# Projection of the second attention as three products of fp32r halves, and a ring of MLP weight pieces with five places

## The chip, the cores and the metric

The kernel runs on one core of a Trainium2 chip. A core has five engines that work at the same time, each through its own list of instructions: TensorE (PE, matmuls and the loads of their weights), VectorE (DVE), ScalarE (ACT), GpSimd (POOL) and SyncE (SP, which here only issues DMAs). They meet through semaphores. The metric is the time on the device of one execution, in microseconds, as the median of some runs.

## The reference

Two layers of gated cross-attention and feed-forward on x, 4 batches of 1024 tokens with 256 features:

```python
x = x + jnp.tanh(g_xattn[0]) * _L0_xattn_ref(_layernorm(x, axis=-1), ctx_1024, ...)   # both ways, with a gate
x = x + jnp.tanh(g_ffn[0]) * _L0_ffn_ref(_layernorm(x, axis=-1), Wr, Wi, Wo)           # 8 experts, the best 2
x = x + jnp.tanh(g_xattn[1]) * _L1_xattn_ref(_layernorm(x, axis=-1), ctx_1024, mask, W, b)
x = x + jnp.tanh(g_ffn[1]) * _L1_ffn_ref(_layernorm(x, axis=-1), w1_w, w1_s, ...)      # 256 -> 1024 -> 1024 -> 1024 -> 256
```

The change is in the third line, the second attention:

```python
x_proj = jax.nn.relu(jnp.einsum('bxd,ed->bxe', x, W) + b)
y_proj = jax.nn.relu(jnp.einsum('byd,ed->bye', y, W) + b)
scores = jnp.einsum('bxd,byd->bxy', x_proj, y_proj)
att = jax.nn.softmax(jnp.where(y_mask[:, None, :], -jnp.inf, scores), axis=-1)
return jnp.einsum('bxy,byd->bxd', att, y)
```

and, through the ring, in the loads of the weights of the fourth line.

## The kernel before

The 4096 tokens are 32 tiles of 128, and 8 groups of 4 tiles (512 tokens). The kernel goes through four stages: A the first attention of all batches; B the experts of the first batch (groups 0 and 1), with all experts' products; C, inside B's last pass and inside the MLP, the second attention of one group at a time; D the MLP, group by group, n = 0 to 7. The experts of the other three batches run inside stage D as well: in groups n = 0, 2, 4 the tokens of the next batch are ranked by expert and their rows scattered to DRAM by GpSimd, loaded again sorted, and multiplied; in groups n = 1, 3, 5 and at their start the results are gathered and added.

Everything in stage D is one list per engine, written out by hand. A group on TensorE is: 8 blocks for the first layers (c = 0 to 7), 16 blocks t = 0 to 15 for the two hidden layers (t = 8 * layer + c, 16 matmuls each), and the output layer. Between blocks stand the pieces of other work. `turn_after(n)` gives the block `at` behind which the second attention of group n + 1 begins: 1 in groups 0, 2, 4, 6, and 5 in groups 1, 3, 5. `c_turn` (transposes of the normalised rows) comes after block `at`, `c_project` after `at` + 1, `c_scores_T` after `at` + 2 and so on. ScalarE's list has its copy out of PSUM (`c_turn`, x_norm_c_T, L1344) after block `at`, VectorE's list the maximum and the update.

The matmuls of the MLP are products of fp32r halves: a value is split into a high part, rounded to fp32r, and a low part, the rest. The weights are small whole numbers that fp32r holds exactly, so the MLP needs 2 products. `c_project` (L889 to L895) is one product of fp32 matmuls with the weight w1t and the transposed rows xcT, 4 matmuls of 128x512. It waits for ScalarE's two copies (semaphore xTc_r).

In groups 0, 2 and 4 VectorE has, in its list, `r_coef` after block t = 0, `r_rank` after t = 1 (L1981 to L2007: a copy of the ranks, then some twenty small instructions, each waiting for the one before; the last one writes slots_of_tokens, for which GpSimd's scatters wait), and `r_tiles` after t = 3.

The MLP's weights are 22 pieces of 512 KB a group. `mlp_ring` has six places (RING); GpSimd loads piece r (`load_piece`, L2210) when the piece that used the place has been read, in its own list, between which stand the scatters (in front of the loads of steps 6 to 9 in groups 0, 2, 4), the update of x (`add`, step 20) and the gathers (at the end of groups 0, 2, 4, and at step 8 of groups 1, 3, 5). In stage B all 22 pieces are examined once by ScalarE (are the weights exact in fp32r?): the first 22 - RING through a buffer of their own that SyncE fills, the last RING in the ring.

Stage B's last pass (`b_last_pass`) has 16 products of experts i on TensorE; VectorE adds their results in 8 steps m (`b_add`). The second attention of group 0 runs through it: `c_turn` after i = 4, `c_project` after i = 6.

Of the kernel before, what the change touches and what calls it, by code (L numbers as in the profile page):

```python
# [27 lines left out]
F32 = mybir.dt.float32  # L28
F32R = mybir.dt.float32r
# [4 lines left out]
ALU = mybir.AluOpType  # L34
# [3 lines left out]
P = 128  # L38
B, S, D, L = 4, 1024, 256, 77
KC = D // P  # L40
# [4 lines left out]
GN = G * P  # L45
# [3 lines left out]
BL = B * L  # L49
NW = (2 * KC + 2 * HC) * HID + HC * D  # L50
PIECE = 1024
RING = 6
ND = 2
NSB = B - 1
EB = 23
# [24 lines left out]
def program(nc, d):  # L80

    ctx = ExitStack()
    with ctx:
# [4 lines left out]
        cursor = {k: v[0] for k, v in room.items()}  # L88
        bytes_of = {U8: 1, U16: 2, BF16: 2}

        def place(region, name, shape, dt=F32, at=None):
            size = int(np.prod(shape[1:])) * bytes_of.get(dt, 4)
            size = -(-size // 32) * 32
            start = cursor[region] if at is None else at
            assert start + size <= room[region][1], (name, start + size)
            cursor[region] = start + size
            return nc.alloc_sbuf_tensor_at(name, shape, dt, offset=base + start)

        def sem(name):
            return ctx.enter_context(nc.semaphore(name))  # L100
# [38 lines left out]
                    at=cursor["weights"] - 2 * KC * BL * 4 + B * 2 * D * 4)  # L139
# [21 lines left out]

        mlp_ring = place("weights", "mlp_pieces", [P, RING, PIECE], F32R, at=wi_at)
        assert NW % PIECE == 0

        xs = place("weights", "slot_rows", [P, 2, CHUNK, D])
        xm = place("weights", "x_norm_of_batch", [P, JT, D], at=cursor["weights"] - 2 * CHUNK * D * 4)
        ys = place("weights", "expert_rows", [P, 2, CHUNK, D])
# [1 line left out]
        xsh = place("weights", "slot_rows_T_high", [P, 2, KC, 2 * P], F32R)  # L169
        xmT = place("weights", "x_norm_T", [P, 2, KC, 2 * P], at=cursor["weights"] - 2 * KC * 2 * P * 4)  # L170
        xsl = place("weights", "slot_rows_T_low", [P, 2, KC, 2 * P], F32R)
        wrb = place("weights", "router_of_batch", [P, KC, E])
        rlg = place("weights", "batch_logits", [P, JT, 2 * E])
        rtop = place("weights", "batch_top8", [P, JT, E])
# [105 lines left out]
        xdl_at = cursor["work"]  # L280
# [4 lines left out]

        xnc = place("work", "x_norm_c", [P, G, D], at=xdh_at)
        xpT = place("work", "x_projected_T", [P, KC, GN], at=xdh_at)
        xcT = place("work", "x_norm_c_T", [P, KC, GN], at=xdl_at)
        scT = place("work", "scores_c_T", [L, GN], at=xdl_at)
        PT = place("work", "probs_c_T", [L, GN], at=ud_at)  # L290
        EC = place("work", "probs_c", [P, G, L])
        w1t = place("work", "context_weight", [P, KC, D])
# [3 lines left out]
        ps = ctx.enter_context(nc.psum_tensor("psum", [P, 8, 512], F32))  # L296
# [85 lines left out]
        yb_r = sem("context_projected_copied")  # L382
        tpc = sem("x_transposed_c_in_psum")
        xnc_r = sem("x_normalised_c_ready")
        xTc_r = sem("x_transposed_c_saved")
        xupc = sem("x_updated_c")
        stats_c = sem("ln_stats_c_ready")
        inv_c = sem("ln_rstd_c_ready")
# [135 lines left out]
        def slot_of(n, piece):  # L524

            return (NCHECK * n + piece) % RING

# [71 lines left out]
        def _(pe):  # L599
            mm = pe.matmul  # L600
# [286 lines left out]
                    transpose_pair(xnc, pair, tpc)  # L887

            def c_project(c):  # L889
                pe.wait_ge(xTc_r, 2 * c + 2)  # L890
                for m in range(KC):
                    for k in range(KC):
                        last = mm(ps[:, 2 + m, :], w1t[:, k, m * P:(m + 1) * P], xcT[:, k, :],  # L893
                                  start=(k == 0), stop=(k == KC - 1))
                    last.then_inc(xp_ps, 1)  # L895

            def c_scores_T(c, b):
# [283 lines left out]
        def _(act):  # L1181
# [159 lines left out]
            def c_turn(c):  # L1341
                for pair in range(2):
                    act.wait_ge(tpc, 1 + pair + 2 * c)
                    act.activation(xcT[:, :, 2 * pair * P:(2 * pair + 2) * P],  # L1344
                                   ps[:, pair, :].rearrange("p (k c) -> p k c", k=KC), ACT.Copy).then_inc(xTc_r, 1)

            def c_project(c):
# [168 lines left out]
        def _(dve):  # L1516
# [342 lines left out]
            def c_norm(c):  # L1859
                dve.wait_ge(inv, INV_A + 1 + c)  # L1860
                for j in range(G):
                    normalise(G * c + j, xnc[:, j, :], xnc_r)

            def c_max(c):
                dve.wait_ge(sb_ps, c + 1)
                dve.tensor_reduce(nmc[:], ps[:, 3, 0:G * L].rearrange("p (j c) -> p j c", j=G), X, ALU.max,
                                  negate=True).then_inc(mc_r, 1)
# [40 lines left out]
            def b_last_pass(g, s):  # L1908

                b_end(g - 1)  # L1910
                c_batch(0)
                for m in range(G * E // 4):
                    b_add(g, s, m)
                    if m == 0:
                        c_norm(0)
                    if m == 3:
                        b_measure(g, 0)
                    if m == 4:
                        c_max(0)
                    if m == 6:  # L1920
                        c_update(0)
                        c_stats(0)
                check_weights()
# [7 lines left out]
            st.mark(dve.memset(rwant[:], FAR))  # L1931
            for t in (Mz, M2, M4, Mc, t1, t2, t4, t8):
                st.mark(dve.memset(t[:], 0.0))
            b_last_pass(ND - 1, 1)


# [110 lines left out]
            def stage_d(short):  # L2047
# [29 lines left out]
                def group(n, b, fetch):  # L2077

                    s, at, a = routed_in(n), turn_after(n), added_in(n)
# [19 lines left out]
                    for layer, (full, part, rest) in enumerate(((hb_f, hb_h, hb_l), (ha_f, ha_h, ha_l))):  # L2099
                        for c in range(HC):  # L2100
                            low(c, full, part, rest, 3 * HC * n + HC * (layer + 1) + c + 1)
                            t = HC * layer + c
# [23 lines left out]
                                    measure_rows(n + 2)  # L2126
                            if b is None:
                                continue
                            if t == at + 3:
                                c_max(n + 1)  # L2130
                            if t == at + 7:
# [220 lines left out]
```

## Time and profile before

| | |
|---|---|
| median of 3 runs | 1082.88 us (1081.75 to 1084.19) |
| profiled execution, own time | 1084.55 us |
| its span | 1082.6 us |
| TensorE busy | 1026.4 us (95%) |
| VectorE busy | 506.4 us (47%) |
| ScalarE busy | 479.9 us (44%) |
| GpSimd busy | 305.6 us (28%) |
| mean granted clock of TensorE | 0.979 |

The profile is one execution, so its own time stands beside the median of the runs. Busy time of TensorE is that of records that overlap; where matmuls follow each other, the distance of their starts says what one costs. The stages in the span: A to about 165 us, B to about 250 us, the MLP stage D from 255 us to the end.

### The profile page before, as it was taken

To read this page: it belongs to the slowest core of one execution; us is meant where nothing else is said; L and a number is where in the kernel's file an instruction comes from. 1 tells how busy PE (TensorE), PEld (TensorE's weight loads), DVE (VectorE), ACT (ScalarE), POOL (GpSimd) and SP (SyncE) were. 2 spreads that over 40 slices of the span, in tenths; PEclk is the share of its full clock that TensorE was granted. 3 is DMA by queue.
4 is the path that set the end of the run, shared out by engine and by line. 5 is a ranking of instruction groups with operands and counts; after the bars stand their busy time and mean duration, and the time that the engine had idled before them with its cause. 6 is when DMAs were issued, how large, how long until landed. Compare 5 with 4: busy or idle time off the path is not lost.

```text
span 1082.6 us, 14392 instructions
## 1 busy us (share of the span) xinstructions
PE 1026.4 (95%) x5218; PEld 831.1 (77%) x5218; DVE 506.4 (47%) x1391; ACT 479.9 (44%) x877; POOL 305.6 (28%) x432
## 2 busy tenths in 40 slices
PE   7989998897999999999999999999999999999996
PEld 4757776665778987886789878867898788788885
DVE  6567766746633362555333624553336245133311
ACT  1345442643544453445444544454445345443431
POOL 0025553311161154222611442225114422012111
PEclk9989998998999999999999999999999999999999
DMA  9930001641266365342663744436637544344540
GB/s 333 375 104 2 2 3 57 220 153 40 83 213 225 137 214 156 117 136 88 224 228 117 228 147 125 125 94 234 210 129 222 156 121 152 117 128 145 152 139 22
DMA packets 44276, 158.93 MB, mean 147 GB/s; under 512 B 6448, under 2 KB 6832, under 8 KB 43306
## 3 DMA queue, kind: packets, MB, share of 16 engines
q0 software_dynamic: 29952, 104.88, 31.1%
q1 hardware_dynamic: 10826, 40.63, 10.9%
q10 hardware_dynamic: 3424, 12.45, 2.9%
q8 instruction: 45, 0.74, 0.3%
q14 instruction: 29, 0.24, 0.1%
HBM read 138.01 MB, written 29.36 MB: 155 GB/s over the span
## 4 chain that ended last, share of the span: by engine, by line
PE 75%; DVE 7%; POOL 6%; ACT 4%; issue 4%; DMA 3%; DVEq 0%; POOLq 0%; ACTq 0%
PE psum L987 48%; POOL slots L2227 4%; PE psum L870 2%; DMA slot_rows<-slots 2%; PE psum L893 2%; PE psum L1064 2%; PE psum L1066 2%; PE psum L1065 2%; PE psum L1040 1%; PE psum L692 1%; PE psum L668 1%; PE psum L706 1%; PE psum L880 1%; PE psum L722 1%; PE psum L605 1%
## 5 line engine op out<-in xcount | busy, mean ns | idle before, releaser
L2214 POOL DMA_DIRECT2D mlp_pieces<-in_mlp x176 | 96.9, 557 | 446.6 <-PE psum L987 440.2
L987 PE MATMUL psum<-hidden_a_high,mlp_pieces 128*128 128x512 f32 x512 | 208.0, 406 | 5.3 <-DVE hidden_a_low L2059 5.3
L987 PE MATMUL psum<-hidden_b_high,mlp_pieces 128*128 128x512 f32 x512 | 202.9, 396 | 0.0
L987 PE MATMUL psum<-hidden_a_low,mlp_pieces 128*128 128x512 f32 x512 | 201.5, 394 | 0.0
L987 PE MATMUL psum<-hidden_b_low,mlp_pieces 128*128 128x512 f32 x512 | 199.7, 390 | 0.0
L2059 DVE TENSOR_TENSOR hidden_a_low<-hidden_a,hidden_a_high 128x512 fp32r<-128x512 f32 x128 | 88.2, 689 | 177.3 <-ACT hidden_a_high L1455 176.7
L2059 DVE TENSOR_TENSOR hidden_b_low<-hidden_b,hidden_b_high 128x512 fp32r<-128x512 f32 x64 | 44.3, 693 | 175.0 <-ACT hidden_b_high L1455 148.2
L987 PEld LDWEIGHTS psum<-hidden_a_high,mlp_pieces 128*128 128x128 f32 x512 | 97.3, 190 | 29.8 <-DVE hidden_a_low L2059 7.6
L987 PEld LDWEIGHTS psum<-hidden_a_low,mlp_pieces 128*128 128x128 f32 x512 | 97.4, 190 | 22.0 <-issue 2.6
L1472 ACT ACTIVATE hidden_a<-psum,mlp_scales 128x512 f32<-128x512 f32 x64 | 44.2, 690 | 156.4 <-PE psum L987 156.3
L987 PEld LDWEIGHTS psum<-hidden_b_high,mlp_pieces 128*128 128x128 f32 x512 | 96.2, 188 | 20.1 <-issue 0.8
L987 PEld LDWEIGHTS psum<-hidden_b_low,mlp_pieces 128*128 128x128 f32 x512 | 96.2, 188 | 19.9 <-issue 0.7
L987 PE MATMUL psum<-x_norm_d_T_high,mlp_pieces 128*128 128x512 f32 x256 | 103.2, 403 | 1.4 <-DVE x_norm_d_T_low L2053 1.4
L987 PE MATMUL psum<-x_norm_d_T_low,mlp_pieces 128*128 128x512 f32 x256 | 101.4, 396 | 0.0
L1472 ACT ACTIVATE hidden_b<-psum,mlp_scales 128x512 f32<-128x512 f32 x64 | 44.2, 690 | 127.8 <-PE psum L987 115.2
L1461 ACT ACTIVATE hidden_a<-psum,mlp_scales 128x512 f32<-128x512 f32 x64 | 44.2, 691 | 95.2 <-PE psum L987 92.7
L1455 ACT ACTIVATE hidden_a_high<-hidden_a 128x512 fp32r<-128x512 f32 x128 | 80.5, 629 | 4.4 <-DVE hidden_a L2084 2.4
L2084 DVE SCALAR_TENSOR_TENSOR hidden_a<-psum,mlp_scales,hidden_a 128x512 f32<-128x512 f32 x64 | 48.1, 751 | 59.5 <-ACT hidden_a L1461 56.0
L987 PE MATMUL psum<-mlp_pieces,hidden_a_high 128*128 128x256 f32 x256 | 63.5, 288 | 2.6 <-DVE hidden_a_low L2059 2.5
L987 PE MATMUL psum<-mlp_pieces,hidden_a_low 128*128 128x256 f32 x256 | 62.2, 283 | 0.0
L987 PEld LDWEIGHTS psum<-x_norm_d_T_high,mlp_pieces 128*128 128x128 f32 x256 | 48.9, 191 | 15.3 <-DVE hidden_a L2084 2.0
L2227 POOL DMA_INDIRECT slots<-x_norm_of_batch,slots_of_tokens x48 | 47.8, 995 | 31.0 <-DVE slots_of_tokens L2006 17.3
(290 smaller groups left out, 1832.0 us busy)
## 6 DMA issues: line engine op xcount, KB each, us to landing
mlp_pieces<-in_mlp POOLq DMA_DIRECT2D x176, 512.0 KB
slots<-in_zeros SPq DMA_DIRECT2D x3, 3072.0 KB, 37.5
yrows<-expert_rows ACTq DMA_DIRECT2D x18, 512.0 KB, 2.7
mlp_piece_to_examine<-in_mlp SPq DMA_DIRECT2D x16, 512.0 KB, 4.4
slot_rows<-slots SPq DMA_DIRECT2D x15, 512.0 KB, 4.9
x_residual<-in_x SPq DMA_DIRECT2D x4, 1024.0 KB, 24.3
out<-x_residual SPq DMA_DIRECT2D x8, 512.0 KB
expert_in<-in_Wi SPq DMA_DIRECT2D x1, 2048.0 KB, 16.0
```

The source lines that it names most:

```text
L870: last = mm(ps[:, 4 + i % 4, :], a[:, s, k, j * P:(j + 1) * P], c[:, k, pair * 2 * D:(pair + 1) * 2 * D], start=(n == 0), stop=(n == 3 * K ...
L893: last = mm(ps[:, 2 + m, :], w1t[:, k, m * P:(m + 1) * P], xcT[:, k, :], start=(k == 0), stop=(k == KC - 1))
L987: last = mm(o, a, b, start=(k == 0 and i == 0), stop=(k == n_k - 1 and i == len(parts) - 1))
L1064: mm(o, xsh[:, q % 2, k, t], wexp_h[:, k, bass.ds(v, D)], start=(k == 0), stop=False)
L1065: mm(o, xsl[:, q % 2, k, t], wexp_h[:, k, bass.ds(v, D)], start=False, stop=False)
L1455: act.activation(part[:, c, :], full[:, c, :], ACT.Copy).then_inc(hi_r, 1)
L1461: act.activation(ha_f[:, c, :], ps[:, d_bank(c), :], ACT.Silu, scale=sc1[:, 0, c:c + 1]).then_inc(sil_r, 1)
L1472: act.activation(full[:, c, :], ps[:, 6 + c % 2, :], ACT.Gelu, scale=sc1[:, 2 + layer, c:c + 1]).then_inc(g_r, 1)
L2059: dve.tensor_tensor(rest[:, c, :], full[:, c, :], part[:, c, :].bitcast(F32), ALU.subtract).then_inc(lo_r, 1)
L2084: dve.scalar_tensor_tensor(ha_f[:, c, :], ps[:, d_bank(c) + 1, :], sc1[:, 1, c:c + 1], ha_f[:, c, :], ALU.mult, ALU.mult).then_inc(h_r, 1)
L2214: pool.dma_start(mlp_ring[:, r % RING, :], d["mlp"][r % NCHECK]).then_inc(ring_in[r % RING], 16)
L2227: pool.indirect_dma_start(slots[s], bass.IndirectOffsetOnAxis(ap=slot[:, s * JT + j, i:i + 1], axis=0), xm[:, j, :], None).then_inc(sc_don ...
```

## The change

The projection of the second attention is made of three products, high times high, low weight times high, and high weight times low, as in the experts. The weight is halved once by VectorE (`halve_context_weight`) before the last pass of stage B. The rows' high half is what ScalarE's copy out of PSUM now writes (as fp32r), and VectorE subtracts it from PSUM for the low half (`c_low`, two instructions). `c_project` waits for these. The place for the halved weight (4 KB in each partition) comes from the ring, which has five places instead of six; the rows' low half lies over the low half of the slot rows.

```diff
-RING = 6
+RING = 5
...
+        w1h = place("weights", "context_weight_high", [P, KC, D], F32R)
+        w1l = place("weights", "context_weight_low", [P, KC, D], F32R)
...
+        xcT_l = place("weights", "x_norm_c_T_low", [P, KC, GN], F32R, at=cursor["weights"] - KC * GN * 4)
...
-        xcT = place("work", "x_norm_c_T", [P, KC, GN], at=xdl_at)
+        xcT_h = place("work", "x_norm_c_T_high", [P, KC, GN], F32R, at=xdl_at)
...
             def c_project(c):
-                pe.wait_ge(xTc_r, 2 * c + 2)
+                pe.wait_ge(xTl_r, 2 * c + 2)
+                if c == 0:
+                    pe.wait_ge(w1_r, 2)
                 for m in range(KC):
                     for k in range(KC):
-                        last = mm(ps[:, 2 + m, :], w1t[:, k, m * P:(m + 1) * P], xcT[:, k, :],
-                                  start=(k == 0), stop=(k == KC - 1))
+                        for i, (w, t) in enumerate(((w1h, xcT_h), (w1l, xcT_h), (w1h, xcT_l))):
+                            last = mm(ps[:, 2 + m, :], w[:, k, m * P:(m + 1) * P], t[:, k, :],
+                                      start=(k == 0 and i == 0), stop=(k == KC - 1 and i == 2))
                     last.then_inc(xp_ps, 1)
...
-                    act.activation(xcT[:, :, 2 * pair * P:(2 * pair + 2) * P],
+                    act.activation(xcT_h[:, :, 2 * pair * P:(2 * pair + 2) * P],
                                    ps[:, pair, :].rearrange("p (k c) -> p k c", k=KC), ACT.Copy).then_inc(xTc_r, 1)
...
+            def c_low(c):
+                for pair in range(2):
+                    dve.wait_ge(xTc_r, 2 * c + pair + 1)
+                    t = slice(2 * pair * P, (2 * pair + 2) * P)
+                    dve.tensor_tensor(xcT_l[:, :, t], ps[:, pair, :].rearrange("p (k c) -> p k c", k=KC),
+                                      xcT_h[:, :, t].bitcast(F32), ALU.subtract).then_inc(xTl_r, 1)
+
+            def halve_context_weight():
+                dve.tensor_copy(w1h[:], w1t[:]).then_inc(w1_r, 1)
+                dve.wait_ge(w1_r, 1)
+                dve.tensor_tensor(w1l[:], w1t[:], w1h[:].bitcast(F32), ALU.subtract).then_inc(w1_r, 1)
...
+                    if m == 2:
+                        c_low(0)
...
+            halve_context_weight()
             b_last_pass(ND - 1, 1)
...
                             if b is None:
                                 continue
+                            if t == at:
+                                c_low(n + 1)
                             if t == at + 3:
                                 c_max(n + 1)
```

Where it moves instructions, as the lists stand. The first place is VectorE in group 0 of stage D (groups 2 and 4 are alike), the end of `r_rank` and what follows. Before:

```order
L2005 SCALAR_TENSOR_TENSOR slot_row<-slot_tile_and_chunk_value,slot_row 128x16
L2006 SCALAR_TENSOR_TENSOR slots_of_tokens<-slot_tile_and_chunk_value,slot_row 128x16
L2059 TENSOR_TENSOR hidden_b_low<-hidden_b,hidden_b_high 128x512 x2
L2012 TENSOR_TENSOR tile_past_expert<-tile_numbers,tiles_so_far 1x184
L2014 TENSOR_REDUCE tile_experts_past<-tile_past_expert 1x23
```

and now:

```order
L2028 SCALAR_TENSOR_TENSOR slot_row<-slot_tile_and_chunk_value,slot_row 128x16
L2029 SCALAR_TENSOR_TENSOR slots_of_tokens<-slot_tile_and_chunk_value,slot_row 128x16
L1876 TENSOR_TENSOR x_norm_c_T_low<-psum,x_norm_c_T_high 128x2x256 x2
L2082 TENSOR_TENSOR hidden_b_low<-hidden_b,hidden_b_high 128x512 x2
L2035 TENSOR_TENSOR tile_past_expert<-tile_numbers,tiles_so_far 1x184
```

The two subtractions of `c_low` stand behind the last instruction of `r_rank` and ahead of the two `low` of blocks t = 2 and 3.

The second place is VectorE before and in the last pass of stage B. Before:

```order
L1933 MEMSET tiles_so_far 128x12
L1532 BN_STATS ln_stats<-x_residual 128x6 x2
L1538 BN_AGGR ln_aggregate<-ln_stats 128x2 x4
L1540 COPY ln_mean_var<-ln_aggregate 128x8
L1856 COPY mask_bias_of_batch<-mask_bias 77x1
L1857 COPY context_projected_of_batch<-context_projected_T 128x154
L1838 SCALAR_TENSOR_TENSOR x_residual<-psum,expert_weight,x_residual 128x256 x4
L1543 TENSOR_SCALAR x_norm_c<-x_residual,ln_mean_var,ln_rstd 128x256 x4
L1838 SCALAR_TENSOR_TENSOR x_residual<-psum,expert_weight,x_residual 128x256 x12
```

and now:

```order
L1955 MEMSET tiles_so_far 128x12
L1880 CAST context_weight_high<-context_weight 128x512
L1882 TENSOR_TENSOR context_weight_low<-context_weight,context_weight_high 128x512
L1540 BN_STATS ln_stats<-x_residual 128x6 x2
L1546 BN_AGGR ln_aggregate<-ln_stats 128x2 x4
L1548 COPY ln_mean_var<-ln_aggregate 128x8
L1864 COPY mask_bias_of_batch<-mask_bias 77x1
L1865 COPY context_projected_of_batch<-context_projected_T 128x154
L1846 SCALAR_TENSOR_TENSOR x_residual<-psum,expert_weight,x_residual 128x256 x4
L1551 TENSOR_SCALAR x_norm_c<-x_residual,ln_mean_var,ln_rstd 128x256 x4
L1846 SCALAR_TENSOR_TENSOR x_residual<-psum,expert_weight,x_residual 128x256 x8
L1876 TENSOR_TENSOR x_norm_c_T_low<-psum,x_norm_c_T_high 128x2x256 x2
```

Two instructions stand ahead of the statistics and of all adds of the pass, and two more behind the third step of adds (m = 2), four adds before where the block of twelve ended.

## Rows read from the trace of the kernel before

**Rows 1.** The page, part 1: busy time, share of the span, instructions.

```profile
PE 1026.4 (95%) x5218; PEld 831.1 (77%) x5218; DVE 506.4 (47%) x1391; ACT 479.9 (44%) x877; POOL 305.6 (28%) x432
```

**Rows 2.** Stretches: span, then each engine's busy time, TensorE's clock, DMA share, GB/s.

```profile
300.00:400.00 100.00, 99.50 (x561) 85.18 (x560) 40.13 (x80) 49.17 (x80) 35.54 (x47) 1.00 0.62 202
```

**Rows 3.** Chain of waits: start, us, what.

```profile
416.44 3.65 PE psum L987 x16
420.09 3.43 PE psum L893 x8
...
498.03 5.32 PE psum L987 x16
```

**Rows 4.** Groups of instructions by shape: the projection (busy us, mean ns).

```profile
L893 PE MATMUL psum<-x_norm_c_T,context_weight 128*128 128x512 f32 x64 | 28.8, 592 | 0.0
```

**Rows 5.** Timeline at the MLP's start: start, us, engine, instruction [idle before].

```profile
253.49 1.41 DVE L2053 TENSOR_TENSOR x_norm_d_T_low<-psum,x_norm_d_T_high 128x512 fp32r<-128x512 f32 x2 [0.55 <-ACT x_norm_d_T_high L1410]
...
254.95 0.80 PE L987 MATMUL psum<-x_norm_d_T_high,mlp_pieces 128*128 128x512 f32 x1 [1.41 <-DVE x_norm_d_T_low L2053]
```

**Rows 6.** Timeline of group 1, before its projection.

```profile
416.86 1.07 ACT L1344 ACTIVATE x_norm_c_T<-psum 128x512 f32<-128x512 f32 x2
...
416.99 0.69 DVE L2059 TENSOR_TENSOR hidden_b_low<-hidden_b,hidden_b_high 128x512 fp32r<-128x512 f32 x1 [1.64 <-ACT hidden_b_high L1455]
...
419.92 3.60 PE L893 MATMUL psum<-x_norm_c_T,context_weight 128*128 128x512 f32 x8
```

**Rows 7.** Timeline of group 0, ScalarE, VectorE and TensorE around its projection.

```profile
289.49 1.07 ACT L1344 ACTIVATE x_norm_c_T<-psum 128x512 f32<-128x512 f32 x2
...
289.62 0.69 DVE L2059 TENSOR_TENSOR hidden_b_low<-hidden_b,hidden_b_high 128x512 fp32r<-128x512 f32 x1 [1.83 <-ACT hidden_b_high L1455]
290.22 0.23 DVE L1984 COPY rank<-psum 128x72 f32<-128x72 f32 x1
...
292.55 3.60 PE L893 MATMUL psum<-x_norm_c_T,context_weight 128*128 128x512 f32 x8
...
294.42 0.69 DVE L2059 TENSOR_TENSOR hidden_b_low<-hidden_b,hidden_b_high 128x512 fp32r<-128x512 f32 x1
```

**Rows 8.** Timeline of group 2, the same place.

```profile
507.69 3.60 PE L893 MATMUL psum<-x_norm_c_T,context_weight 128*128 128x512 f32 x8
...
509.56 0.69 DVE L2059 TENSOR_TENSOR hidden_b_low<-hidden_b,hidden_b_high 128x512 fp32r<-128x512 f32 x1
```

**Rows 9.** Waits of TensorE: for whom, us in total, times, longest.

```profile
PE psum L1040 <- DMA slot_rows<-slots: 0.6, 2, 0.4
```

**Rows 10.** Stretches of TensorE in group 2: busy time, clock, DMA share, GB/s.

```profile
494.60:498.06 3.46, 1.53 (x8) 1.00 0.07 25
498.06:501.48 3.42, 3.42 (x9) 0.50 0.56 158
```

**Rows 11.** Timeline of TensorE at the start of stage B's last pass.

```profile
217.44 0.50 PE L870 MATMUL psum<-expert_high,x_T_high 128*128 128x512 f32 x1 [2.59 <-DVE x_residual L1838]
```

**Rows 12.** Groups of VectorE by shape: a cast and a copy.

```profile
L1591 DVE CAST score_bias_repeated<-score_bias_rows 2x308 fp32r<-2x308 f32 x4 | 1.2, 300 | 0.0
L1626 DVE COPY attention_weights<-psum 128x512 f32<-128x512 f32 x1 | 0.7, 691 | 0.3 <-PE psum L653 0.3
```

**Rows 13.** Timeline of stage B's last pass, before its projection.

```profile
223.01 1.88 DVE L1838 SCALAR_TENSOR_TENSOR x_residual<-psum,expert_weight,x_residual 128x256 f32<-128x256 f32 x4 [1.94 <-PE psum L870]
...
224.20 3.59 PE L893 MATMUL psum<-x_norm_c_T,context_weight 128*128 128x512 f32 x8
```

**Rows 14.** Timeline of group 1: loads behind the gathers, the first hidden block.

```profile
391.85 1.74 POOL L2214 DMA_DIRECT2D mlp_pieces<-in_mlp  x3
...
393.55 0.39 PE L987 MATMUL psum<-hidden_a_high,mlp_pieces 128*128 128x512 f32 x1
```

**Rows 15.** Stretches of group 1, all engines, clock, DMA share, GB/s last.

```profile
393.00:396.00 3.00, 3.00 (x15) 2.50 (x14) 2.42 (x5) 2.06 (x5) 1.13 (x3) 1.00 0.95 268
393.00:398.00 5.00, 5.00 (x24) 3.99 (x23) 3.03 (x5) 3.82 (x6) 1.43 (x4) 1.00 1.02 315
```

More of the change, by code:

```diff
@@ L384, in program @@
         xnc_r = sem("x_normalised_c_ready")
-        xTc_r = sem("x_transposed_c_saved")
+        xTc_r = sem("x_transposed_c_high_saved")
+        xTl_r = sem("x_transposed_c_low_saved")
+        w1_r = sem("context_weight_halves_ready")
         xupc = sem("x_updated_c")
```

## The prediction, made before the changed kernel was run

> **What bounds the kernel now.** I read the page first: TensorE is busy for 95% of the span, VectorE for 47% [rows 1]. One matmul more or less is time; work on VectorE is free only while no matmul waits for it. Then a stretch of a hundred microseconds in the MLP stage, which takes the last three quarters of the span: TensorE is busy for 99.5% of it [rows 2]. Then the chain of waits. Through the MLP stage it runs along TensorE itself, blocks of 16 matmuls in 3.65 us with the projection of the second attention between them [rows 3]. So a group of this stage ends when TensorE has issued its list. What I looked for last, in the timeline, is what stands on VectorE and ScalarE just before each of the eight projections, because the change makes each wait for two more VectorE instructions.
>
> **The matmuls.** Before, a projection is 4 fp32 matmuls, recorded as 8 pieces (64 in all, [rows 4]), and takes 3.43 us on the chain [rows 3]. After, it is 12 matmuls of fp32r halves with the same 128x512 form as the MLP's. Sixteen of those take 3.65 us [rows 3], 0.228 each, so 12 take 2.74. Each projection is shorter by 0.68 us and the eight by **5.4**.
> The Trainium skill, "FP8 and Floating Point Precision", section "TensorE Precision Notes", counts true fp32 as four passes through the array. By passes alone three instead of four would take a quarter of the time away, 0.86 us a projection and 6.9 in all; the row of the fp32r blocks says 0.68, and the row decides.
>
> **The low half, in groups 1, 3, 5 and 6.** `c_low` is two subtractions from PSUM of 128x512. The MLP's own instruction of this form takes 0.69 us, and the one behind it starts 0.60 us after it [rows 7], so the pair takes 1.30. TensorE starts 0.05 us after such a pair ends [rows 5]. In group 1 ScalarE ends its two copies at 417.93 and VectorE's own `low` ends at 417.68; the pair ends by about 419.2 and the projection starts at 419.92 [rows 6]. The 16 matmuls between transposes and projection hide it, with 0.7 us to spare. Groups 3, 5 and 6 have the same order. Cost 0; without that cover it would be 1.3 each time.
>
> **The low half, in groups 0, 2 and 4.** Here the order decides. In these groups the transposes come after block t = 1, and on VectorE block t = 1 also carries `r_rank`, the chain of some twenty small instructions that ranks the tokens of a batch. `c_low` stands behind it in the list (the order rows of the change show it between `slots_of_tokens` and the next `hidden_b_low`). In group 0 `r_rank` starts at 290.22 and VectorE comes to the next instruction at 294.42, while the projection starts at 292.55, and ScalarE's copies are done at 290.56 [rows 7]. The pair takes that place: 294.42 + 1.30 + 0.05 = 295.77, so TensorE waits 3.22 us. In group 2 it is 509.56 + 1.35 against 507.69, again 3.22 [rows 8]; group 4 repeats the distances. That is 3 x 3.22 = **+9.7**. Queued behind the waiting matmuls is the whole rest of the group, and nothing there catches up, except one wait: at the first transposes of the scattered rows TensorE waits for the DMA of the slots, 0.6 us over all groups [rows 9]. GpSimd's scatters hang on `slots_of_tokens`, which comes before `c_low` and is not moved, so these waits go: **-0.6**. The `hidden_b_low` behind the pair is late by 1.2 us; the second hidden layer, which reads it, starts some 20 us later.
>
> **The clock after such a wait.** In group 2 TensorE was busy 1.53 us of a stretch of 3.46 at full clock, and in the next 3.42 us the granted clock was 0.50, its lower level of 1.2 GHz [rows 10]. The block of 16 that starts there takes 5.32 instead of 3.65 us: 1.67 lost [rows 3]. Group 4 shows the same; group 0, with nearly the same wait, does not. The new wait is longer, 3.22 us in one piece. Bounds per wait: 0 and 1.67. I take 1.37 for each of the three, because a part of the half-clock stretch can lie in the idle time itself: **+4.1**.
> The Trainium skill, "TensorE: Matmul & The Clock Gate", section "HAM oscillation — how this bites in real kernels", has a kernel whose matmuls start throttled after every wait for data, with half of the throttled time lost. By that rule each of the three waits costs the full 1.67 and the sum is 0.9 us higher; the trace has it after two of three shorter waits.
>
> **The last pass of the experts (before the MLP stage).** Two edits. `halve_context_weight` adds a copy and a subtraction of 128x512 in SBUF behind the memsets. After them come statistics and the adds to x_residual for which TensorE stands idle 2.59 us until 217.44 [rows 11], so this is on the path. The subtraction is 0.60 until the next instruction. The copy lies between 0.30 (a cast of 308 elements in SBUF) and 0.69 (a copy of 512 from PSUM) [rows 12]; I take 0.4, nearer to the one in SBUF. With 0.1 for the semaphore between them: **+1.1**, bounds 1.0 and 1.4. And `c_low(0)` stands behind the third group of adds. Four adds start at 223.01 and take 1.88 us, three of them ahead of it, so it starts at about 224.42 and ends at 225.72; the projection goes from 224.20 to about 225.8 [rows 13]: **+1.6**.
>
> **The ring of five.** Each piece is now asked for one block of 3.65 us later. In steady state it is requested four blocks (14.6 us) before its use. The tight place is behind GpSimd's eight gathers at the start of groups 1, 3, 5: three loads are issued from 391.85 on [rows 14]. Before, the first of them is piece 6; after, it is piece 5, for the second hidden block, which starts at 393.55 + 3.65 = 397.2 [rows 14]. The DMA moves 0.80 MB from 393 to 396 [rows 15], and a piece is 0.52, so the first is through before 395.5: 1.7 us to spare. In the even groups the loads between the scatters come 7 us and more before use. Cost 0, upper bound in rival 2. The examined slices stay 22. ScalarE's copy with an fp32r output replaces one with fp32 output; it has 0.7 us of cover too. Cost 0.
>
> **The sum.** -5.4 + 9.7 - 0.6 + 4.1 + 1.1 + 1.6 = **+10.5 us**. Against the profiled execution of 1084.55 this is 1095.1. That execution lies 1.7 above the median of the three runs, 1082.88, as much as one stretch at half clock costs; so the forecast for a median is **1093.4**.
>
> **Rivals.** (1) *The waits come, but the clock stays up*, as after group 0's wait: 4.1 less, 1089.3. For it: one of three; against it: the new wait is longer.
> (2) *The ring is a bound too*: piece 5 counts as landed only with its two followers. Three pieces are 1.57 MB, and from 393 to 398 the DMA moves 5 x 315 = 1.58 [rows 15]: 398.0, 0.8 us late, in three groups, +2.4, and another fall of the clock is not excluded (up to +5): 1095.8 to 1100.8. For it: the DMA engines are fully busy there; against it: one queue serves its requests in order.
> (3) *Other side, faster*: `c_low` is hidden everywhere, as in group 1. The sum is then -5.4 + 1.1 = -4.3, 1078.6. VectorE would have to be free by 291.2 in group 0, 3.2 us before `r_rank` ends; from there on it decides. Only the margin of group 1 speaks for it.
> (4) *No change*: the slots' DMA ends the even groups, not TensorE's list, and swallows their waits. Then -0.68 x 5 + 1.1 + 1.6 = -0.7 remains: 1082.2. Against it: the wait there is 0.6 us over all groups [rows 9]; it can't swallow 9.7.
>
> **How the numbers follow.** Forecast 0.70 (its own range 1091 to 1096: the copy's bounds, none or the full 1.67 in one of the three waits, and the existing falls of the clock, which may come or go with the shifted times), rival 1 0.15, rival 2 0.08, rival 3 0.04, rival 4 0.03. The range reaches over rival 1 and into rival 2: 1088 to 1098. A change below about 0.2% (2.2 us) can't be told from none, so slower is 0.70 + 0.15 + 0.08 = 0.93, same 0.03, faster 0.04.
>
> **What would show it.** 96 matmuls of the projection, 12 each time in 2.74 us; in groups 0, 2, 4 a wait of TensorE of about 3.2 us for `x_norm_c_T_low`, none in groups 1, 3, 5, 6, one of 1.6 in the last pass; a granted clock of 0.50 soon behind the long ones; no wait for slot rows and none for `mlp_pieces`. I am wrong if the pair runs ahead of `slots_of_tokens`, if TensorE waits for pieces at about 397, or if 12 matmuls take 3.4 us.

## The result, and the profile after

The changed kernel takes 1095.85 us (median of 6 runs, 1093.3 to 1100.36), the kernel before 1084.62 in the same series (6 runs, 1081.75 to 1087.29): a ratio of 1.0105, 95% interval 1.0084 to 1.0126, or 11.2 us slower. The forecast was 10.5 us slower, 1093.4 us. The profiled execution of the changed kernel is one of 1096.94 us, span 1095.0, mean granted clock 0.972 (before: 1084.55, 1082.6, 0.979). One execution of e4b below took 1830.69 us at a granted clock of 0.75; it is in no median and no ratio.

Part 1 of the page, as in [rows 1]:

```profile
PE 1028.2 (94%) x5250; PEld 843.0 (77%) x5250; DVE 516.5 (47%) x1409; ACT 478.6 (44%) x877; POOL 305.0 (28%) x432
```

TensorE has hardly more to do than before, though its products are shorter: the difference of 12 us in the span is time in which it waits or runs at the lower clock. The waits of TensorE (for whom, us in total, times, longest):

```profile
PE psum L901 <- DVE x_norm_c_T_low L1876: 10.3, 4, 3.0
...
PE psum L875 <- DVE x_residual L1846: 3.7, 1, 3.7
```

There is no row for slot rows any more, where [rows 9] had 0.6 us, and none for MLP pieces. The chain of waits, all eight projections (as in [rows 3]):

```profile
230.60 3.03 PE psum L901 x12
301.54 4.61 PE psum L901 x12
429.62 2.72 PE psum L901 x12
519.66 4.41 PE psum L901 x12
647.55 2.72 PE psum L901 x12
736.01 4.59 PE psum L901 x12
863.98 2.72 PE psum L901 x12
940.43 2.72 PE psum L901 x12
```

Where TensorE comes to the projection without a wait, the 12 matmuls take 2.72 us. Behind the waits of groups 0, 2 and 4 they take 4.4 to 4.6. In the kernel before, the chain has only five of the eight projections. In groups 0, 2 and 4 it leaves TensorE behind the ranking and goes through GpSimd's scatters and the DMA of the slot rows; this is its part in group 0:

```profile
294.79 1.24 POOL slots L2227
...
315.92 2.56 DMA slots<-x_norm_of_batch,slots_of_tokens
318.49 8.02 DMA slot_rows<-slots
326.56 1.09 PE psum L1040 x8
```

So in these three groups TensorE's list and the slot rows were ready at nearly the same time. In the changed kernel TensorE comes later, and the chain stays with it. The timeline of group 0 shows the order that makes the wait (as [rows 7]):

```profile
295.29 1.07 ACT L1352 ACTIVATE x_norm_c_T_high<-psum 128x512 fp32r<-128x512 f32 x2
...
300.12 0.17 DVE L2029 SCALAR_TENSOR_TENSOR slots_of_tokens<-lot_tile_and_chunk_value,slot_row 128x16 int32<-128x16 f32 x1
300.21 1.28 DVE L1876 TENSOR_TENSOR x_norm_c_T_low<-psum,x_norm_c_T_high 128x512 fp32r<-128x512 f32 x2
...
301.54 0.50 PE L901 MATMUL psum<-x_norm_c_T_high,context_weight_high 128*128 128x512 f32 x1 [3.03 <-DVE x_norm_c_T_low L1876]
```

ScalarE has saved the high rows at 296.4; the pair starts at 300.21, right behind the last instruction of the ranking, and TensorE starts 0.05 us after its end. Groups 2 and 4 have the same rows with idle times of 3.02 and 3.04. Stretches of TensorE in groups 0 and 2 (span, length, busy time of the engines, granted clock, DMA share, GB/s; as [rows 10]):

```profile
299.08:302.49 3.41, 0.95 (x4) 0.82 (x5) 2.83 (x11) 0.78 (x2) 1.61 (x2) 1.00 0.10 35
302.49:305.90 3.41, 3.41 (x10) 2.64 (x9) 0.00 (x0) 0.69 (x1) 2.80 (x4) 0.50 0.25 85
517.46:520.87 3.41, 1.21 (x5) 1.03 (x6) 2.61 (x9) 0.57 (x1) 1.87 (x2) 1.00 0.11 38
520.87:524.28 3.41, 3.41 (x9) 2.63 (x9) 0.00 (x0) 0.85 (x2) 2.73 (x4) 0.51 0.25 89
```

TensorE was busy for 0.95 and 1.21 us of the first stretch of each pair, and in the second its granted clock was half, 1.2 GHz. Group 4 is the same from 736.04 on.

The last pass of stage B, VectorE's halving and TensorE's start (as [rows 11]), and the stretches of TensorE behind it:

```profile
217.10 0.41 DVE L1880 CAST context_weight_high<-context_weight 128x512 fp32r<-128x512 f32 x1
...
217.55 0.69 DVE L1882 TENSOR_TENSOR context_weight_low<-context_weight,context_weight_high 128x512 fp32r<-128x512 f32 x1
...
221.26 0.79 PE L875 MATMUL psum<-expert_high,x_T_high 128*128 128x512 f32 x1 [3.69 <-DVE x_residual L1846]
```

```profile
220.50:223.90 3.40, 2.64 (x6) 2.04 (x7) 3.40 (x10) 0.00 (x0) 3.40 (x6) 0.51 0.74 237
223.90:227.30 3.40, 3.40 (x13) 3.02 (x12) 0.95 (x3) 1.97 (x3) 0.17 (x1) 0.50 0.90 296
```

TensorE's wait there is 3.69 us, 1.10 more than in [rows 11], and the half clock behind it lasts 6.8 us. In the kernel before it was 3.4 us; these are its stretches:

```profile
218.20:221.60 3.40, 3.40 (x13) 2.92 (x12) 2.87 (x8) 0.69 (x2) 2.62 (x5) 0.50 1.03 339
221.60:225.00 3.40, 3.40 (x14) 2.44 (x13) 1.75 (x4) 1.54 (x3) 0.00 (x0) 1.00 1.09 386
```

From the timelines of the two executions I read how much later the same instruction starts; the last column is what a part added:

| start of | before | after | later | added |
|---|---|---|---|---|
| first memset ahead of the last pass | 213.74 | 216.46 | 2.72 | 2.72 |
| transposes of x_norm_d, group 0 | 251.57 | 257.39 | 5.82 | 3.10 |
| the same, group 1 | 372.20 | 381.65 | 9.45 | 3.63 |
| group 2 | 463.64 | 472.44 | 8.80 | -0.65 |
| group 3 | 587.12 | 599.74 | 12.62 | 3.82 |
| group 4 | 678.57 | 690.38 | 11.81 | -0.81 |
| group 5 | 802.20 | 816.07 | 13.87 | 2.06 |
| group 6 | 893.64 | 906.80 | 13.16 | -0.71 |
| group 7 | 985.41 | 997.76 | 12.35 | -0.81 |

The first 2.72 us lie in stages that the change doesn't touch: this execution was at half clock there for 27.3 us, the one before for 20.5. The 2.06 of group 4 would be 3.7: the kernel before had a half-clock stretch at 713 us, worth 1.6, that this one has not.

### The profile page after: what moved, and what is told of

Same layout as the page of the kernel before. It is cut to its first block, busy times and chain, and to the rows that moved or that the text cites. A ratio compares the mean times of both kernels' runs of the same rounds, so it can differ in the third digit from the quotient of the medians.

```text
span 1095.0 us, 14476 instructions
## 1 busy us (share of the span) xinstructions
PE 1028.2 (94%) x5250; PEld 843.0 (77%) x5250; DVE 516.5 (47%) x1409; ACT 478.6 (44%) x877; POOL 305.0 (28%) x432
## 4 chain that ended last, share of the span: by engine, by line
PE 82%; DVE 9%; ACT 4%; issue 2%; POOL 1%; DMA 1%; DVEq 0%; SPq 0%; POOLq 0%; ACTq 0%
PE psum L995 55%; PE psum L901 3%; PE psum L875 2%; PE psum L1072 2%; PE psum L1074 2%; PE psum L1073 2%; PE psum L1048 1%; PE psum L697 1%; PE psum L673 1%; PE psum L927 1%; PE psum L909 1%; PE psum L711 1%; PE psum L885 1%; DMA x_residual<-in_x 1%; PE psum L727 1%
## 5 line engine op out<-in xcount | busy, mean ns | idle before, releaser
L995 PE MATMUL psum<-hidden_a_high,mlp_pieces 128*128 128x512 f32 x512 | 204.4, 399 | 5.3 <-DVE hidden_a_low L2082 5.3
L995 PEld LDWEIGHTS psum<-x_norm_d_T_low,mlp_pieces 128*128 128x128 f32 x256 | 48.9, 191 | 8.8
```

The source lines that it names most:

```text
L995: last = mm(o, a, b, start=(k == 0 and i == 0), stop=(k == n_k - 1 and i == len(parts) - 1))
```

## The experiments

The experiments were timed in five rounds beside the kernel before: 1083.81 us (19 runs) for the first four, 1085.34 (22 runs) for the next four, 1084.43 (23 runs) for the last two. The changed kernel's row is the result above. I compare by the ratio to the kernel before; 0.001 is 1.08 us, and the last column is the ratio in us (for the changed kernel 11.4, where the difference of the two medians is 11.2).

| kernel | median us (runs) | ratio to before | us |
|---|---|---|---|
| changed kernel | 1095.85 (6) | 1.0105 [1.0084, 1.0126] | +11.4 |
| e1, low half ahead of the ranking | 1090.30 (6) | 1.0056 [1.0036, 1.0076] | +6.1 |
| e2, projection a block later | 1088.95 (6) | 1.0053 [1.0038, 1.0068] | +5.7 |
| e3, ring of five alone | 1084.98 (12) | 1.0009 [0.9995, 1.0023] | +1.0 |
| e4, no low rows | 1086.98 (8) | 1.0023 [1.0005, 1.0041] | +2.5 |
| e5, matmuls in the wait | 1089.83 (11) | 1.0050 [1.0032, 1.0067] | +5.4 |
| e7, halving in idle time | 1093.31 (6) | 1.0075 [1.0052, 1.0097] | +8.1 |
| e3b, ring of four alone | 1098.87 (5) | 1.0136 [1.0110, 1.0163] | +14.7 |
| e9, halves in groups 1, 3, 5, 6 only | 1080.99 (12) | 0.9960 [0.9944, 0.9976] | -4.3 |
| e8, e2 and e7 in one | 1085.35 (12) | 1.0008 [0.9993, 1.0022] | +0.9 |
| e4b, e4 and e7's halving | 1083.33 (11) | 0.9997 [0.9985, 1.0009] | -0.3 |

**e1: the low half ahead of the ranking.**

```diff
+                            if s is not None and t == at:
+                                c_low(n + 1)
                             if s is not None and t == 1:
                                 r_rank(s)
...
-                            if t == at:
+                            if t == at and s is None:
                                 c_low(n + 1)
```

> In groups 0, 2 and 4 the two subtractions of c_low stand ahead of r_rank instead of behind it; nothing else differs from the changed kernel. If the order on VectorE is what costs: TensorE's waits of 3.0 us for x_norm_c_T_low in these groups go, with the half clock behind them; in their place slots_of_tokens comes 1.2 us later, and TensorE waits some 2 us at the slot rows. Each of the three groups is then about 1.3 us longer than in the kernel before instead of 3.7: 1096 - 7 = about 1089 us, up to 4 more if the clock falls behind the new wait. If the extra time is the ring's or the matmuls' own, nothing moves: 1096.

The waits for x_norm_c_T_low in stage D are gone, so the place in VectorE's list is what made them. Others stand in their place, TensorE's for the slot rows:

```profile
PE psum L1048 <- DMA slot_rows<-slots: 7.6, 3, 3.0
```

The ranking ends later by the pair, the scatters start later, and TensorE comes to the slot rows sooner. The three waits are 3.02, 2.51 and 2.02 us, where I had 2 us each. Only the second has half clock behind it. The one of 3.02 us in group 0, as long as those of the changed kernel, has not; the last 3.41 us before it ends and the next 3.41:

```profile
329.45:332.86 3.41, 0.39 (x3) 0.01 (x1) 0.69 (x1) 1.32 (x2) 0.53 (x1) 1.00 1.09 405
332.86:336.27 3.41, 3.41 (x19) 2.99 (x20) 2.09 (x5) 1.09 (x2) 0.00 (x0) 1.00 0.77 284
```

**e2: the projection a block later.**

```diff
         def turn_after(n):
+            if routed_in(n) is not None:
+                return 2
             return 1 if added_in(n) is None else 5
```

(with `c_attend` of these groups ahead of the slot rows' transposes, as before.)

> In groups 0, 2 and 4 the whole second attention begins one block later (block 2 instead of 1), so that 16 more matmuls lie between r_rank and the projection; c_attend stays ahead of the first slot rows. Order theory: no wait for x_norm_c_T_low in stage D, no wait of GpSimd's scatters more than before; the groups then last as long as before (TensorE's 0.7 us less is waited for at the slot rows). Sum against the kernel before: -0.68 x 5 + 1.1 + 1.6 = -0.7, about 1084 us, 12 less than the changed kernel. Rival (the waits move elsewhere, or the ring): 1090 or more.

No wait for x_norm_c_T_low in stage D, and the ranking undisturbed. The waits for slot rows are 3.2 us in all instead of 0.6. By the ratio the time is 6.4 us above my sum of -0.7, so the bound of my rival (1090 or more) is nearer than my forecast. The trace explains a part: the last pass is 3.08 us longer than before where the sum had 2.0, and TensorE's wait of 1.85 us for the slot rows in group 0 has a half-clock stretch behind it, worth 1.7. This trace is of the fastest of the six executions (1084.53 us; the others took 1088.4 to 1090.1), so it doesn't show what made the others slower. e7 and e8 bear on the last pass.

**e3: the ring of five alone** (kernel before, RING = 5).

> The kernel before with five places of the ring in use; the projection is the old one and all addresses stay. My theory: 0, 1084.6 us, no wait of TensorE for mlp_pieces. Ring theory: up to +5, with waits of about 1 us in groups 1, 3, 5 at the second hidden block.

Same time within its interval, and no matmul waits more than 0.16 us for a piece.

**e4: no low rows.** The rows' low half is left out of the computation; the third product takes the high rows again, so the 12 matmuls stay.

```diff
-                pe.wait_ge(xTl_r, 2 * c + 2)
+                pe.wait_ge(xTc_r, 2 * c + 2)
...
-                        for i, (w, t) in enumerate(((w1h, xcT_h), (w1l, xcT_h), (w1h, xcT_l))):
+                        for i, (w, t) in enumerate(((w1h, xcT_h), (w1l, xcT_h), (w1h, xcT_h))):
...
-                            if t == at:
-                                c_low(n + 1)
```

> The changed kernel without c_low: the third product takes the rows' high half again, so the rows' low half is left out of the result; 12 matmuls a projection, the halving of the weight and the ring of five stay. If a projection of 12 halves is 0.68 us shorter: the kernel before - 0.68 x 5 (groups 0, 2, 4 give theirs back at the slot rows) + 1.1 = -2.3 to -4.3, 1080.5 to 1082.5 us. If the halves are no cheaper than fp32: 1085.5 or more.

Every wait for the low half is gone, 9 us against the changed kernel, but 5 us of what I expected are missing. The timelines give three places. The last pass is still 1.70 us longer than before, with the projection 0.68 shorter: 2.4 us are VectorE's 1.1 for the halving and, in this execution, a second half-clock stretch behind TensorE's wait of 3.70 us. Groups 0, 2 and 4 hand their 0.68 back, in longer waits for the slot rows: 1.83, 1.01 and 0.84 us. And group 0 has a half-clock stretch from 288 on, which the kernel before has not.

**e5: matmuls in the wait.** As soon as the high rows are there, TensorE does 13 matmuls of no use in groups 0, 2, 4, and then waits.

```diff
+                if routed_in(c - 1) is not None:
+                    pe.wait_ge(xTc_r, 2 * c + 2)
+                    for _ in range(13):
+                        mm(ps[:, 5, :], w1h[:, 0, 0:P], xcT_h[:, 0, :], start=True, stop=True)
                 pe.wait_ge(xTl_r, 2 * c + 2)
```

> The changed kernel, with 13 dummy matmuls (high weight, high rows, into bank 5, overwritten later) issued by TensorE in groups 0, 2 and 4 as soon as the high rows are saved, so that it works through the 3.0 us in which it waited for x_norm_c_T_low. Theory: the 3.2 us of delay in each of three groups stay, and the half-clock stretch behind each goes: about 4.4 us less than the changed kernel, 1091.5 against 1095.9. Rival, that the half-clock stretches come however TensorE spends those 3 us: no less than the changed kernel, 1095 to 1097.

The same stretches of group 2 as above, in e5 (the first is busy with the end of a block and the useless matmuls):

```profile
514.05:517.46 3.41, 3.41 (x17) 2.83 (x16) 3.10 (x21) 1.32 (x2) 0.34 (x1) 1.00 0.01 2
517.46:520.87 3.41, 3.31 (x15) 2.42 (x14) 1.17 (x2) 0.69 (x1) 2.72 (x3) 1.00 0.22 77
```

The projection starts as late as in the changed kernel, at full clock. From its transposes to those of the slot rows the three groups are 2.12, 2.33 and 2.17 us longer than in the kernel before; the changed kernel has 3.69, 3.90 and 3.76 there. So the idle time costs 4.7 us in clock, 1.6 a group, on top of itself. The rival is out. The medians say 6.0.

**e7: the halving in idle time, c_low(0) a step earlier.**

```diff
+            dve.wait_ge(fin, NT)
+            halve_context_weight()
             dve.wait_ge(inv, INV_A)
-            dve.wait_ge(fin, NT)
...
-                    if m == 2:
+                    if m == 1:
                         c_low(0)
...
-            halve_context_weight()
             b_last_pass(ND - 1, 1)
```

> The changed kernel, with the halving of the context weight ahead of the wait for GpSimd's ln_rstd, in which VectorE stood idle for 1.5 us before, and c_low(0) one step earlier in the last pass. Theory: the 1.1 us of the halving ahead of the last pass and the longer half-clock stretch behind them are the +3.1 by which that pass came out later; with both gone the projection alone is left, 0.68 shorter: about 3.8 less than the changed kernel, 1092. Rival, that the +3.1 are the wait for x_norm_c_T_low in the last pass: 1.1 to 1.5 less, 1094.5.

From the first memset to the transposes of x_norm_d e7 is 0.68 us shorter than the kernel before, exactly the projection; the changed kernel is 3.10 longer. Two edits are made at once here, so the 3.78 are those of both. VectorE and TensorE of e7:

```profile
215.39 0.42 DVE L1880 CAST context_weight_high<-context_weight 128x512 fp32r<-128x512 f32 x1
215.85 0.69 DVE L1882 TENSOR_TENSOR context_weight_low<-context_weight,context_weight_high 128x512 fp32r<-128x512 f32 x1
217.51 0.17 DVE L1953 MEMSET batch_logits<- 128x128 f32 x1 [0.97 <-POOL ln_rstd L2199]
```

```profile
221.80:225.20 3.40, 3.40 (x14) 2.83 (x12) 2.65 (x8) 0.47 (x1) 2.27 (x4) 0.50 0.87 271
225.20:228.60 3.40, 3.40 (x17) 2.81 (x16) 3.23 (x7) 1.76 (x4) 0.00 (x0) 1.00 0.95 318
```

There is still idle time in front of the memset after both instructions, and the half clock is back to one stretch. The time is 3.3 less than that of the changed kernel; the rival's 1.1 to 1.5 is too little for the profile. The medians lean the same way, but their intervals don't exclude it.

**e3b: the ring of four alone** (kernel before, RING = 4).

> The kernel before with four places in the ring of MLP pieces, one fewer than the changed kernel has. Theory: piece 4 can be fetched only when the first hidden block has left piece 0, so the place is missed where the pieces are loaded behind a group: its load lands about 2 us late in groups 1, 3 and 5, three waits for mlp_pieces of 2 us, up to 1.5 of half clock behind each: 6 to 10 us more than before, 1090 to 1094. Rival, that the ring has places to spare even so: no wait, 1084.

14.7 us slower, where I had 6 to 10. The wait of TensorE and its price in group 1, from the timeline and the chain of waits:

```profile
392.14 1.74 POOL L2214 DMA_DIRECT2D mlp_pieces<-in_mlp  x3
```

```profile
397.01 0.80 PE L987 MATMUL psum<-hidden_a_high,mlp_pieces 128*128 128x512 f32 x1 [2.96 <-DMA mlp_pieces<-in_mlp]
```

```profile
392.14 4.82 DMA mlp_pieces<-in_mlp
...
611.77 5.34 DMA mlp_pieces<-in_mlp
...
830.62 4.76 DMA mlp_pieces<-in_mlp
```

A piece lands 4.8 to 5.3 us after its issue behind the gathers. I had reckoned with 3.65, so the three waits are 10.4 us in all and not 6, and in group 1 the half clock behind the wait lasts 6.8 us and not 3.4:

```profile
PE psum L987 <- DMA mlp_pieces<-in_mlp: 10.4, 3, 4.0
```

That number bears on the ring of five too (below).

**e9: the halves in groups 1, 3, 5 and 6 only.** The last pass and groups 0, 2, 4 keep the fp32 projection; the halving stands in group 0 behind block t = 4.

```diff
+        LOWS = [2, 4, 6, 7]
+        def whole(c):
+            return c not in LOWS
...
+                if whole(c):
+                    pe.wait_ge(xTc_r, 2 * c + 2)
+                    for m in range(KC):
+                        for k in range(KC):
+                            last = mm(ps[:, 2 + m, :], w1t[:, k, m * P:(m + 1) * P], xcT[:, k, :],
+                                      start=(k == 0), stop=(k == KC - 1))
+                        last.then_inc(xp_ps, 1)
+                    return
+                pe.wait_ge(xTl_r, 2 * LOWS.index(c) + 2)
...
+                            if n == 0 and t == 4:
+                                halve_context_weight()
-                            if t == at:
+                            if t == at and not whole(n + 1):
+                                c_low(n + 1)
```

> The three products only for x_norm_c of the stages that follow groups 1, 3, 5 and 6, where the rows' low half is ready in time; in the last pass of B and in groups 0, 2 and 4 the four-pass fp32 projection of the kernel before; the halving in VectorE's idle time in group 0; ring of five. Theory: 4 x 0.68 less than the kernel before, nothing given back: 1083.8 - 2.7 = 1081.1. Rival, that the low half's subtraction costs VectorE something there too, or that the halving in group 0 delays something: 1083 to 1085.

This beats both kernels. In the timelines groups 1, 3, 5 and 6 are each 0.73 or 0.74 us shorter than in the kernel before from the transposes of x_norm_c on, 2.9 in all. Over the whole group it is 0.76, 0.49, 0.76 and 0.78: in group 3 TensorE's weight load waited 0.44 us for a piece of the ring of five. In group 0 TensorE waits 0.5 us longer for the slot rows; beside that half-clock stretches come and go, as in every execution. The halving lies at 308.92 and costs TensorE nothing.

**e8 and e4b: the two cures together.**

> e2 and e7 in one: in groups 0, 2 and 4 the turn, the low half and the projection of x_norm_c a block later, and the halving of the context weight in VectorE's idle 1.5 us, c_low(0) one step earlier. Theory: the two cures are of different places and add up: e2 stood at 1.0053 of before (5.8 us above it), the last pass gives 3.8 back as in e7, so 2 us above before, ratio 1.002. Rival, that e2's median was high for a reason in the groups that this shift does not touch and that the last pass repays no more than the 1.1 us of VectorE: ratio 1.004 or more. Rival the other way, that all three groups are free as in e2's profiled run: 3.4 us under before, ratio 0.997.

> e4 (the rows' low half left out, the third product takes the high rows again) with the halving of the context weight in VectorE's idle 1.5 us. Theory: e4 missed its 1081.5 by 5 us for three reasons: the halving ahead of the last pass with the half-clock stretch behind it (2.4 us), the 0.68 of each even group handed back at the slot rows (2.0 us), and the rest in half-clock stretches. With the halving hidden the time falls by 2.4: ratio 1.0023 - 0.0022 = 1.000. Rival, that the halving costs VectorE's 1.1 us alone: ratio 1.0013. Rival, that nothing stands between the shorter products and the end once it is gone: 5.4 under before less the 2.0 at the slot rows, ratio 0.997.

e8 is 4.8 us under e2, e4b 2.8 under e4, where the theory had 3.8 and 2.4: the cures add up. But the sums of e2 and e4 had 2.7 and 1.1 us for the last pass already, so the last pass explains some 2 us of each of their misses, of 6.4 and 4.8. e8 is still 4.3 us above the gain of 3.4 of its last rival. In its trace one group is long, group 0, by 2.6 us against the kernel before; there and in group 2 TensorE waits longer for the slot rows:

```profile
PE psum L1050 <- DMA slot_rows<-slots: 4.1, 3, 1.9
```

and behind the one in group 0, 1.90 us, is a half-clock stretch, from 329.3 on. In e4 and e4b TensorE waits 1.83 and 1.86 us at the same place and keeps its full clock. The rest of e8's median is not explained.

## Why the prediction was right

- **The matmuls.** 2.74 us forecast, 2.72 measured, and 0.65 to 0.81 saved in each group without a wait. The row of the MLP's own fp32r blocks was the right one.
- **Groups 1, 3, 5, 6.** No wait for the low half. In group 1 the pair ends at 428.41, 1.0 us before the projection. Shown by e9: there the shorter projection is kept whole.
- **Groups 0, 2, 4.** Forecast 3.22 us of delay at the projection; the timelines give 3.19 each time (5.80 to 8.99 late in group 0). Shown by e1 and e2: with the pair ahead of the ranking, or the projection a block later, this wait goes.
- **The slot rows.** Their waits went, as forecast. But I read the chain of waits as running along TensorE through the whole stage; in the kernel before it goes through the DMA of the slot rows in groups 0, 2 and 4, the path that rival 4 names. The sum did not suffer, since the new wait of TensorE is longer than that path had to spare. It is why e2 and e4 hand their 0.68 back in these groups.
- **The clock.** Forecast 1.37 for each of the three; from the projection to the slot rows the delay grows by 0.50, 0.71 and 0.57 more although the projection gives 0.68 back, and in groups 0 and 4 the old waits of 0.36 and 0.26 go too. So the clock cost 1.54, 1.39 and 1.51, 4.4 in all against 4.1. Shown by e5, with 4.7. Rival 1 is out for this kernel. The Trainium skill ("TensorE: Matmul & The Clock Gate", section "HAM oscillation — how this bites in real kernels") has a kernel whose matmuls start throttled after every wait for data, with half of the throttled time lost. All three waits here were followed by half clock, and each cost 1.4 to 1.6 us of some 3.4; e7 has the same three waits with the same behind them. But e1's wait of 3.02 us was not followed by any, so three out of three was likely and not certain, and a part of the agreement in this term is luck. My reason for taking 1.37, that a part of the stretch can lie in the idle time, did not hold: TensorE was busy in all of it.
- **The last pass: a term was left out.** Forecast +1.1 for the halving, +1.6 for the wait for the low half, -0.68: +2.0. Measured +3.10. The halving did cost VectorE's 1.1, and the copy 0.41 as taken; the wait for the low half was 1.17. But TensorE's wait of 2.59 us in the kernel before had a half-clock stretch behind it already, and behind the wait of 3.69 us came two. I priced the clock behind new waits and not behind an old one that grew. e7 takes the halving and the low half's wait away together and gets 3.78 back; e4 finds 2.4 of it without any wait for the low half. The second stretch doesn't come in every execution. e1, e2 and e5 have the same last pass, and TensorE waits 3.64 to 3.71 us there; e2 has two stretches and is 3.08 us longer than before, e1 and e5 have one and are 1.75 and 1.73 longer, about what I had forecast. e1's:

```profile
221.70:225.10 3.40, 3.36 (x10) 2.71 (x11) 3.40 (x10) 0.00 (x0) 2.88 (x5) 0.52 0.67 188
225.10:228.50 3.40, 3.40 (x18) 2.66 (x16) 1.48 (x5) 2.12 (x4) 0.00 (x0) 0.98 1.04 354
```

- **The ring: right time, wrong margin.** I gave piece 5 1.7 us to spare in groups 1, 3 and 5. In the changed kernel its load is issued at 401.28, and the first weights of its block are loaded

```profile
406.66 0.19 PEld L995 LDWEIGHTS psum<-hidden_a_high,mlp_pieces 128*128 128x128 f32 x1 [0.19 <-DMA mlp_pieces<-in_mlp]
```

  5.4 us after the issue, with the piece as the last thing waited for. The margin is nothing. TensorE lost less than 0.1 us here, but in e3 its matmul waited 0.16 us in group 3, in e1 0.87 in group 1, and in e7 0.89 in group 1:

```profile
405.25 0.50 PE L995 MATMUL psum<-hidden_a_high,mlp_pieces 128*128 128x512 f32 x1 [0.89 <-DMA mlp_pieces<-in_mlp]
```

  What failed is the estimate from the DMA's rate over a stretch: it tells when the bytes could be through, not when TensorE may read them. e3b shows the landing time by itself. Rival 2 was nearer than its 0.08 says.
- **The sum** came out as 11.2 between medians against 10.5. The interval goes from 9.1 to 13.7 us, so medians that agree to 0.7 are partly luck. The profiled executions differ by 12.4, of which 2.7 lie ahead of the change and -1.6 is the half-clock stretch at 713 that did not come. The 11.3 that remain are 3.1 for the last pass (forecast 2.0), 11.1 for groups 0, 2 and 4 (forecast 11.2) and -3.0 for groups 1, 3, 5 and 6 (forecast -2.7).

Open: in e5 the medians give 6.0 back where the timelines find 4.7, within the intervals. What brings and takes half-clock stretches in the stages that no kernel here changes was not followed. Nor is it shown why one wait of TensorE has half clock behind it and another as long has not: 1.85 and 1.90 us at the slot rows of group 0 had (e2, e8), 1.83 and 1.86 at the same place had not (e4, e4b).

## What to carry to other kernels

The same instruction can be free in one group and cost 3 us in the next, because of what stands ahead of it on its engine: look for the longest chain of small instructions in front of each new producer. Price a wait of TensorE with the clock behind it, about 1.5 us for most of some 3 us here, give the chance that it stays away a price too, and look also at old waits that the change makes longer. Look for the second path that ends a stage at nearly the same time: what TensorE saves ahead of it comes back as waiting. Where an order can't be mended without a new wait, use the cheaper operation only where its operands are there in time, as e9 does; and take the spare time of a load from a landing that the trace shows.

## What the runs showed of the hardware

- 12 matmuls of fp32r 128x512 take 2.72 us, 0.227 each; 4 fp32 ones of the same shape took 3.43 before, 0.86 each. Three for one saves 21%.
- VectorE copies 128x512 fp32 to fp32r within SBUF in 0.41 us; the subtraction with an fp32r result takes 0.69, from PSUM and in SBUF alike.
- Useless matmuls in the waits of 3 us kept the clock up in groups 0, 2 and 4 and gained 1.6 us each time (e5).
- Waits of TensorE of 3.0 us were followed by half clock in all six places of the changed kernel and e7 and not in e1 (3.02 us); waits of 3.64 to 3.71 us at the last pass were followed by 6.8 us of it in three traces (changed kernel, e2, e4) and by 3.4 us in two (e1, e5).
- A 512 KB load issued by GpSimd behind eight gathers landed 4.8 to 5.4 us after its issue (e3b, changed kernel).
